# An attention and feed-forward block on one core: all eight PSUM banks in one pool, value products in two halves of the queries, and the normalisation moved from TensorE transposes to transfers and GpSimd

## The chip, the cores and the metric

The kernel runs on one core of a Trainium2 chip. The metric is the device time of one execution in microseconds (us), lower is better. The core has TensorE (PE in the profile, PEld its weight loads), VectorE (DVE), ScalarE (ACT), GpSimd (POOL) and SyncE (SP), which here only issues transfers (DMA). Each engine works through its own list of instructions in order and waits on semaphores for the others. TensorE writes its results into PSUM, which has eight banks of 512 f32 numbers in each of 128 partitions; the other tiles lie in SBUF.

## The reference

For x of 16 batches x 1024 positions x 256 features, with six modulation rows for each batch out of a small product (silu(c) @ w_mod):

```python
h = layernorm(x) * (1 + ca) + sa
Q, K, V = (h @ w.T + b, split into 16 heads of 16)
scores = Q @ K.T / 4 + slope[head] * (k_pos - q_pos), causal
out = softmax(scores) @ V
x = x + ga * (out @ o_w.T + o_b)
h = layernorm(x) * (1 + cb) + sb
gate, y = fp4(h) @ fp4(w_gate).T, fp4(h) @ fp4(w_up).T
x = x + gb * (fp4(silu(gate) * y) @ fp4(w_down).T)
```

fp4 rounds blocks of 16 numbers to a grid of eight magnitudes times the scale of the block. ga and gb are kept at least 0.25 in magnitude.

## The kernel before

The 16 heads are worked on in four groups (g) of four heads (G = 4). For each batch b there are five strands of work, which overlap across batches:

- projections, one batch ahead: N1, N2, N3 (VectorE) normalise x; TR transposes it (TensorE) and ScalarE copies it into featT; U are the query and key projections and V the values. SPL (GpSimd) splits queries and keys into three bf16 parts, and MOVE (SP, six transfers for each unit and group) brings the parts under each other into qa and ka.
- maxima, up to a group ahead: S (TensorE, L655) computes scores with the queries on the partitions, VectorE takes the maximum of each row (L1018, L1020), SM and MT turn the maxima round and TOP (SP) writes them into qa.
- attention: T (L619 to L622) computes the scores again, transposed, ScalarE takes the exponential (L815) into `probs` (three slots in `arena`), and PV (L635) multiplies by the values. The values have a 17th column of ones, so a 17th row of each head's output is the sum of its exponentials. A group has 12 steps (kt, c): kt is one of 8 tiles of keys, c the half of the queries (512 columns); kt of 4 and more meet only c = 1, by causality. Each step issues four products, one for each head, at partitions 0, 32, 64 and 96 of the accumulator `o_acc`, which has two PSUM banks of its own, one for each half.
- after each group: CO (ScalarE, L802) copies o_acc into oT, ON (TensorE, L671) transposes it in eight tiles into two banks, and VectorE takes the reciprocal of the sums (L1044) and multiplies into otok (L1046), which has positions on the partitions. After the fourth group OT (TensorE, L701) transposes otok back in 16 tiles, ScalarE copies it into featT (L834), and O (L711) is the output projection.
- feed forward: LR, LN normalise; XR, XQ, HR, HQ are the fp4 rounding on VectorE and GpSimd (L937, L940), XT and HT transposes, GA (L730), UP (L737) and DN (L753) the three products, RES adds the residual on GpSimd and OUT stores. The residual of the next batch (XIN, FOLD) is loaded into xr behind it.

The order on each engine is written out before the kernel is built: `plan()` adds every job with a cost, a due time and the jobs that it comes after, and `Plan.settle()` puts them one by one, always the one that can start earliest, and among those the one due first. The other six PSUM banks are given out there too: `banks` is how many neighbouring banks a job of TensorE takes, and the job on the other engine that empties them gives them back. Three rings bound how many jobs an engine may have waiting: A (TensorE to ScalarE, four), D (TensorE to VectorE, two) and Q (VectorE to GpSimd, two). A batch is planned at L = 240 us. On the chip `open_banks(e)` waits until the last owners of the banks have emptied them; no job is reordered.

Of the kernel before, what the change touches and what calls it, by code (L numbers as in the profile page):

```python
# [7 lines left out]
ALU = mybir.AluOpType  # L8
# [7 lines left out]
P = 128  # L16
BANK = 512
# [27 lines left out]
STEPS = [(kt, c) for kt in range(T) for c in range(2) if c == 1 or kt < T // 2]  # L45
# [3 lines left out]
NT = len(TILES)  # L49
DIAGONAL = [s for s, (kt, c) in enumerate(STEPS) if c == kt // (T // 2)]  # L50
# [28 lines left out]
class Plan:  # L79
# [5 lines left out]
    BANKS, AHEAD = 6, {"A": 4, "D": 2, "Q": 2}  # L85

    def __init__(self):
        self.jobs, self.order = {}, {e: [] for e in ("PE", "ACT", "DVE", "POOL", "SP")}
        self.bank, self.before = {}, {}

    def add(self, engine, event, cost, due, *after, lag=0.06, ring=None, takes=None, lock=None, banks=0):


        self.jobs[engine, event] = (cost, due, [a for a in after if a], lag, ring, takes, lock, banks)

    def settle(self):
# [29 lines left out]
        while ready:  # L126
# [36 lines left out]
            if banks:  # L163
# [3 lines left out]
                owner[first:first + banks] = [(self.RINGS[ring][1], event)] * banks  # L167
# [15 lines left out]
def plan():  # L183
# [9 lines left out]
    def projections(b, at):  # L193
# [51 lines left out]
    def attention(b, at):  # L245
        n, last = 0, ("PE", ("T", b - 1, NG - 1, NS - 1, jobs_of(NS - 1) - 1))
        for g in range(NG):
            for s in range(NS):
                w = span(s)[1]
                heads = together(s)  # L250
                for i in range(jobs_of(s)):
# [7 lines left out]
                    n += heads  # L259
                p.add("PE", ("PV", b, g, s), 1.9e-3 * w + 0.03, due + 3, ("ACT", ("T", b, g, s, jobs_of(s) - 1)),  # L260
                      ("PE", ("PV", b, g, s - 1)) if s else None, ("ACT", ("CO", b, g - 1) if g else ("CO", b - 1, NG - 1)) if s == 0 else None,
                      ("DVE", ("V", b, 1)) if (g, s) == (0, 0) else None,
                      ("PE", ("ON", b, g - 1) if g else ("ON", b - 1, NG - 1)) if s == NS - 1 else None, lag=0.22)
# [15 lines left out]
    def feed_forward(b, at):  # L279

        for c in range(C):
            for hf in range(2):
                pe(("OT", b, c, hf), 0.55, at + 1.0, ("DVE", ("ON", b, NG - 1)), ("PE", ("V", b + 1, 1)), ring="A", on="ACT",
                   takes_cost=0.59)
        for r in range(NPAIR):
            pe(("O", b, r), 1.75, at + 2.0 + r, ("ACT", ("OT", b, 0, r // 2)), ("ACT", ("OT", b, 1, r // 2)), ("POOL", ("WG", b)),
# [53 lines left out]
def adaln_block(nc, x, wq, bq, wk, bk, wv, bv, wo, bo, w_gu, w_down, cond, w_mod, out):  # L340
    start_slope = 2.0 ** (-8.0 / H)
    slopes = [start_slope * start_slope ** i for i in range(H)]
    rows_dram = nc.dram_tensor("rows_dram", (B, 4 * D), F32).ap()

    with ExitStack() as ctx:
# [7 lines left out]
        o_acc = ctx.enter_context(nc.psum_tensor("o_acc", [P, 2 * BANK], F32))  # L353
# [14 lines left out]
        otok = sb("otok", [P, T, D])  # L368
# [28 lines left out]
        rden = [sb(f"rden{n}", [P, T, G]) for n in range(2)]  # L397
# [7 lines left out]
        wraw2 = otok[:, :, :].rearrange("p t f -> p (t f)")  # L405
# [4 lines left out]
        slope_row = sb("slope_row", [1, 8, H])  # L410
        slope_col = sb("slope_col", [P, H])
        is_a, is_b = sb("is_a", [P, 1]), sb("is_b", [P, 1])
# [7 lines left out]
        o_free = sem("o_free")  # L420
# [36 lines left out]
        def _(sp):  # L457
# [75 lines left out]
            for r in range(NPAIR):  # L533
                sp.wait_ge(stored[r], 16 * B)
# [699 lines left out]
```

## Time and profile before

| | |
|---|---|
| median of 3 runs | 4182.7 us (4179.85 to 4183.4) |
| the profiled execution | 4182.51 us |
| its span, first to last instruction | 4180.7 us |
| mean granted clock of TensorE | 0.967 |
| TensorE busy | 3731.8 us (89%), 22068 matmuls |
| VectorE busy | 3130.8 us (75%) |
| ScalarE busy | 1946.8 us (47%) |
| GpSimd busy | 1196.2 us (29%) |
| bytes moved by transfers | 169.89 MB |

The chain of work that ended last lies for 73% of the span on TensorE, 13% on VectorE and 9% on ScalarE. Busy times of an engine leave out its waits; the busy time of a group of instructions counts overlapping instructions once.

### The profile page before, as it was taken

Reading aid. Unit: us, or ns where it says so; the run is one execution under the profiler, and the core shown is the slowest. Engines: PE = TensorE matmul, PEld = TensorE weight load, DVE = VectorE, ACT = ScalarE, POOL = GpSimd, SP = SyncE. Lnnn points to the kernel's source line nnn. Section 1 sums busy time; section 2 is a strip of 40 time slices with the busy share of each in tenths; the row PEclk is TensorE's granted clock in tenths of the full one; section 3 lists DMA queues with packets and bytes.
Section 4 is the critical chain, followed back from the end, with each engine's and each line's share of the span. In section 5 each row is a group of like instructions: output and inputs, shape, how many; then the busy total and the mean of one; then the engine's idle time right before and its main releaser. Section 6 shows DMA issues by size and latency. Waiting matters only on the chain.

```text
span 4180.7 us, 58634 instructions
## 1 busy us (share of the span) xinstructions
PE 3731.8 (89%) x22068; PEld 1974.5 (47%) x22068; DVE 3130.8 (75%) x6125; ACT 1946.8 (47%) x3535; POOL 1196.2 (29%) x886
## 2 busy tenths in 40 slices
PE   1799999999989989999999999999999998999886
PEld 0334454454545445454544545445454544544445
DVE  7477768778786787877777786777877688776855
ACT  2255444544444554444444454454544455445441
POOL 2222314132231323223132331423224132321223
PEclk6799999999999999999999999999999999999997
DMA  2532122213122122212213122222212212212000
GB/s 76 71 57 33 39 43 45 40 34 51 30 48 45 28 46 41 49 34 46 43 29 52 34 44 46 37 41 37 51 31 52 46 25 49 41 27 45 11 15 10
DMA packets 127981, 169.89 MB, mean 41 GB/s; under 512 B 22020, under 2 KB 75988, under 8 KB 127700
## 3 DMA queue, kind: packets, MB, share of 16 engines
q1 hardware_dynamic: 127700, 166.15, 22.8%
q8 instruction: 176, 2.88, 0.3%
q14 instruction: 105, 0.86, 0.1%
HBM read 47.01 MB, written 16.84 MB: 15 GB/s over the span
## 4 chain that ended last, share of the span: by engine, by line
PE 73%; DVE 13%; ACT 9%; issue 2%; SPq 1%; DMA 1%; POOL 1%; DVEq 0%; ACTq 0%; POOLq 0%
PE o_acc L635 13%; PE banks L655 10%; PE banks L619 9%; PE banks L753 8%; PE banks L730 7%; PE banks L737 7%; ACT arena L815 7%; PE banks L686 4%; PE banks L711 3%; PE banks L694 3%; PE banks L746 2%; DVE banks L1020 2%; DVE tm L993 2%; PE banks L622 1%; PE banks L671 1%
## 5 line engine op out<-in xcount | busy, mean ns | idle before, releaser
L815 ACT ACTIVATE arena<-banks 128x512 f32<-128x512 f32 (+1 forms) x2432 | 1289.4, 576 | 1239.7 <-PE banks L622 702.9
L1020 DVE CUSTOM_DVE_ANT_0 banks<-banks,mask 128x640 f32<-128x640 f32 (+3 forms) x1024 | 1038.0, 1040 | 228.1 <-PE banks L655 218.3
L619 PE MATMUL banks<-qa,ka 105*128 105x512 bf16 (+3 forms) x3072 | 852.3, 332 | 154.3 <-ACT arena L815 125.4
L655 PE MATMUL banks<-ka,qa 102*128 102x512 bf16 (+3 forms) x3072 | 761.6, 334 | 104.7 <-DVE top L1020 80.1
L635 PE MATMUL o_acc<-arena,va 128*17 128x512 f32 (+3 forms) x6144 | 642.4, 500 | 13.1 <-ACT arena L815 12.5
L619 PEld LDWEIGHTS banks<-qa,ka 105*128 105x128 bf16 x3072 | 280.2, 98 | 674.1 <-ACT arena L815 471.2
L655 PEld LDWEIGHTS banks<-ka,qa 102*128 102x128 bf16 x3072 | 267.1, 99 | 484.8 <-DVE top L1020 150.9
L1018 DVE TENSOR_REDUCE top<-banks 128x2 f32<-128x768 f32 (+3 forms) x384 | 391.6, 1043 | 138.5 <-PE banks L660 107.8
L937 POOL TENSOR_TENSOR hid<-hid,tm 128x704 f32<-128x704 f32 x128 | 214.7, 1678 | 900.1 <-DVE hid L994 900.1
L753 PE MATMUL banks<-wdT,hqT 128*128 128x256 f32 x1536 | 371.2, 393 | 3.6 <-ACT hqT L846 3.2
L730 PE MATMUL banks<-wguT,xqT 128*128 128x352 f32 x1024 | 337.0, 463 | 2.8 <-ACT hqT L846 2.0
L737 PE MATMUL banks<-wguT,xqT 128*128 128x352 f32 x1024 | 328.4, 464 | 1.6 <-DVE top L1020 1.2
L753 PEld LDWEIGHTS banks<-wdT,hqT 128*128 128x128 f32 x1536 | 293.4, 195 | 73.6 <-ACT hqT L846 15.1
L622 PE MATMUL banks<-maskT,identb 128*128 128x128 bf16 x1536 | 323.4, 222 | 0.0
L945 POOL TENSOR_TENSOR xr<-xr,delta 128x256 f32<-128x256 f32 x128 | 93.0, 727 | 615.7 <-DVE delta L1123 615.7
L841 ACT ACTIVATE hid<-banks 128x352 f32<-128x352 f32 x256 | 118.5, 463 | 305.7 <-PE banks L730 305.3
L1117 DVE TENSOR_TENSOR hid<-hid,banks 128x704 f32<-128x704 f32 x128 | 113.5, 887 | 191.6 <-PE banks L737 181.9
L737 PEld LDWEIGHTS banks<-wguT,xqT 128*128 128x128 f32 x1024 | 189.3, 190 | 106.6 <-DVE top L1020 4.2
L730 PEld LDWEIGHTS banks<-wguT,xqT 128*128 128x128 f32 x1024 | 183.0, 191 | 100.7 <-ACT hqT L846 6.5
L635 PEld LDWEIGHTS o_acc<-arena,va 128*17 128x17 f32 x6144 | 108.2, 96 | 251.7 <-issue 147.9
L937 POOL TENSOR_TENSOR xb<-xb,tm 128x512 f32<-128x512 f32 x64 | 81.3, 1270 | 457.8 <-DVE xb L994 457.8
L1123 DVE TENSOR_TENSOR delta<-banks,ffn_rows 128x256 f32<-128x256 f32 x128 | 54.2, 423 | 199.9 <-PE banks L753 137.0
(148 smaller groups left out, 4929.5 us busy)
## 6 DMA issues: line engine op xcount, KB each, us to landing
qa<-parts SPq DMA_DIRECT2D x384, 128.0 KB, 4.6
ka<-parts SPq DMA_DIRECT2D x384, 128.0 KB, 6.2
xa<-in_x SPq DMA_DIRECT2D x16, 1024.0 KB, 5.2
xr<-in_x SPq DMA_DIRECT2D x64, 256.0 KB, 2.8
out_x<-xr SPq DMA_DIRECT2D x64, 256.0 KB, 2.1
ffn_rows<-rows_dram SPq DMA_DIRECT2D x16, 384.0 KB, 4.2
ga_row<-rows_dram SPq DMA_DIRECT2D x16, 128.0 KB, 2.9
qa<-in_w_mod SPq DMA_DIRECT2D x2, 768.0 KB, 5.6
```

Source lines behind the costliest of these rows:

```text
L619: mm = pe.matmul(ps[:, m * w:(m + 1) * w], ka[g][0:KT, h, kt * P:(kt + 1) * P], qa[g][0:KT, h, q0:q0 + w], start=heads < G, stop=heads == ...
L622: mm = pe.matmul(ps[:, m * w:m * w + P], identb[:, :], maskT[:, :], start=False, stop=True, skip_group_check=True)
L635: mm = pe.matmul(o_acc[32 * h:32 * h + VW, q0:q0 + w], va[:, kt, g * G + h, :], probs[:, s % P_SLOTS, h, 0:w], start=(kt == 0), stop=(kt = ...
L655: mm = pe.matmul(ps[:, at:at + z - a], qa[g][0:KS, h0 + m, qt * P:(qt + 1) * P], ka[g][0:KS, h0 + m, a:z], start=qt > 0, stop=qt == 0 or h ...
L686: mm = pe.matmul(ps[:, :], w[:, c, m * P:(m + 1) * P], featT[:, c, hf * BANK:(hf + 1) * BANK], start=(c == 0), stop=(c == C - 1))
L730: mm = pe.matmul(ps[:, 0:FH], src[:, c, :], wguT[:, c, e[3] * FH:(e[3] + 1) * FH], start=(c == 0), stop=(c == C - 1))
L737: mm = pe.matmul(ps[:, k * BANK:k * BANK + FH], src[:, c, :], wguT[:, c, FF + k * FH:FF + (k + 1) * FH], start=(c == 0), stop=(c == C - 1))
L753: mm = pe.matmul(ps[:, 0:D], hqT[t % 2][:, c, :], wdT[:, c, :], start=(c == 0), stop=(c == FC - 1))
L815: nc.scalar.activation(probs[:, s % P_SLOTS, j * heads:(j + 1) * heads, 0:w], ps[:, 0:heads * w].rearrange("p (h q) -> p h q", h=heads), A ...
L937: nc.gpsimd.tensor_tensor(u, u, m, ALU.subtract).then_inc(gridded, 1)
L1018: nc.vector.tensor_reduce(tops, ps, AX.X, ALU.max).then_inc(d_free, 1)
L1020: nc.vector.tensor_tensor_reduce(out=ps, in0=ps, in1=mask[:, S - w:S], scale=1.0, scalar=MASKED, op0=ALU.add, op1=ALU.max, accum_out=tops) ...
```

## The change

PSUM: `o_acc` is gone, `banks` has all eight. A half of the queries takes one bank with its first PV (`FIRST`) and holds it until its own copy CO (`holder`) has been made after its last PV (`LAST`). The steps run first over the four tiles of keys of half 0, then over the eight of half 1. Ring D may have three jobs waiting, and the maxima are due 30 us ahead instead of 20.

Normalisation: ON and OT go, and with them otok and its reciprocals. oT keeps the features on the partitions, as O needs them. For each group SP issues DEN (the four rows of sums out of oT into 128 partitions x 32), VectorE takes the reciprocal (RD), SP writes them to DRAM (RDW) and reads them back spread over 64 partitions (RBC, into rsumT); NUM, four transfers, brings the 4 x 16 rows of outputs together in onT. For each two groups GpSimd multiplies onT by rsumT (MUL, 128 x 1024). O reads onT and waits for both MULs of the batch. CO waits until DEN and NUM of the group before have landed. O no longer reads featT, and TR no longer waits for an earlier O.

At the start VectorE clears all eight banks first, where it cleared o_acc, and the first transposes wait for it; some small tiles of the start share space.

```diff
-STEPS = [(kt, c) for kt in range(T) for c in range(2) if c == 1 or kt < T // 2]
+STEPS = [(kt, c) for c in range(2) for kt in range((c + 1) * T // 2)]
+FIRST, LAST = (0, T // 2), (T // 2 - 1, NS - 1)
...
-    BANKS, AHEAD = 6, {"A": 4, "D": 2, "Q": 2}
+    BANKS, AHEAD = 8, {"A": 4, "D": 3, "Q": 2}
...
-                owner[first:first + banks] = [(self.RINGS[ring][1], event)] * banks
+                owner[first:first + banks] = [self.holder[event]] * banks
...
-                pe(("TR", b, c, hf), 0.5, at + 0.08 * L + c, ("DVE", ("N3", b, 1)), ("PE", ("O", b - 2, NPAIR - 1)),
-                   ("PE", ("V", b - 1, 1)), ring="A", on="ACT", takes_cost=0.8)
+                pe(("TR", b, c, hf), 0.5, at + 0.08 * L + c, ("DVE", ("N3", b, 1)), ("PE", ("V", b - 1, 1)), ring="A", on="ACT", takes_cost=0.8)
...
-                due = at + L * n / (NG * sum(h * (q + 1) * P for q, _, h in TILES)) - 20.0
+                due = at + L * n / (NG * sum(h * (q + 1) * P for q, _, h in TILES)) - 30.0
...
-            p.add("ACT", ("CO", b, g), 1.2, due, ("PE", ("PV", b, g, NS - 1)))
-            pe(("ON", b, g), 1.2, due + 6, ("ACT", ("CO", b, g)), ("PE", ("OT", b - 1, C - 1, 1)), ring="D", on="DVE",
-               takes_cost=1.15, banks=2, then=(("DVE", ("ON", b, g - 1)),) if g else ())
+                      banks=1 if s in FIRST else 0, holder=("ACT", ("CO", b, g, c)) if s in FIRST else None)
+                if s in LAST:
+                    past = (b, g - 1) if g else (b - 1, NG - 1)
+                    p.add("ACT", ("CO", b, g, c), 0.6, due, ("PE", ("PV", b, g, s)), ("SP", ("NUM", *past)), ("SP", ("DEN", *past)))
+            normalise(b, g, due)
+
+    def normalise(b, g, due):
+
+        old = (b, g - 1) if g else (b - 1, NG - 1)
+        done = [("ACT", ("CO", b, g, c)) for c in range(2)]
+        p.add("SP", ("DEN", b, g), 0.7, due, *done, ("DVE", ("RD", *old)), lag=2.5)
+        p.add("SP", ("NUM", b, g), 2.6, due + 1, *done, ("PE", ("O", b - 1, NPAIR - 1)), lag=3.0)
+        p.add("DVE", ("RD", b, g), 0.4, due, ("SP", ("DEN", b, g)), ("SP", ("RDW", *old)))
+        p.add("SP", ("RDW", b, g), 0.7, due, ("DVE", ("RD", b, g)), ("SP", ("RBC", *old)), lag=2.5)
+        p.add("SP", ("RBC", b, g), 0.7, due, ("SP", ("RDW", b, g)), ("POOL", ("MUL", b, g // 2 - 1) if g >= 2 else ("MUL", b - 1, C - 1)), lag=3.0)
+        if g % 2:
+            p.add("POOL", ("MUL", b, g // 2), 2.2, due + 10.0, *((("SP", (k, b, n)) for n in (g - 1, g) for k in ("NUM", "RBC"))))
...
+                        sp.dma_start(sums[:, :], oT[HD:P:P // G, :]).then_inc(sums_in, 16)
...
+                        for h in range(G):
+                            sp.dma_start(onT[half + HD * h:half + HD * (h + 1), g // 2, :],
+                                         oT[P // G * h:P // G * h + HD, :]).then_inc(outputs_in, 16)
...
+                    sp.dma_start(rsum_dram[g].rearrange("h (p q) -> (h p) q", q=G * S // P), rsums[:, :]).then_inc(rsums_out, 16)
...
+                    sp.dma_start(rsumT[half:half + 64, :], rsum_dram[g].unsqueeze(1).broadcast_to((G, HD, S))).then_inc(rsumT_in, 16)
...
-                            mm = pe.matmul(o_acc[32 * h:32 * h + VW, q0:q0 + w], va[:, kt, g * G + h, :],
-                                           probs[:, s % P_SLOTS, h, 0:w], start=(kt == 0),
-                                           stop=(kt == (c + 1) * (T // 2) - 1), skip_group_check=True)
+                            mm = pe.matmul(out[32 * h:32 * h + VW, :], va[:, kt, g * G + h, :],
+                                           probs[:, s % P_SLOTS, h, 0:w], start=s in FIRST,
+                                           stop=s in LAST, skip_group_check=True)
...
                         if r == 0:
+                            pe.wait_ge(normal, b * C + C)
                             pe.wait_ge(wog_ready, b + 1)
...
-                                mm = pe.matmul(ps[:, j * D:(j + 1) * D], featT[:, c, t * P:(t + 1) * P], wog[:, c, :],
+                                mm = pe.matmul(ps[:, j * D:(j + 1) * D], onT[:, c, t * P:(t + 1) * P], wog[:, c, :],
...
-                        act.wait_ge(pv_done, (b * NG + e[2] + 1) * NS)
-                        for c in range(2):
-                            nc.scalar.copy(oT[:, c * BANK:(c + 1) * BANK], o_acc[:, c * BANK:(c + 1) * BANK]).then_inc(o_free, 1)
+                        _, _, g, c = e
+                        n = b * NG + g
+                        act.wait_ge(pv_done, n * NS + LAST[c] + 1)
+                        if n:
+                            act.wait_ge(outputs_in, 64 * n)
+                            act.wait_ge(sums_in, 16 * n)
+                        nc.scalar.copy(oT[:, c * BANK:(c + 1) * BANK], bank(("PV", b, g, FIRST[c]))).then_inc(o_free, 1)
...
+                        nc.gpsimd.tensor_tensor(onT[:, c, :], onT[:, c, :], rsumT[:, :], ALU.mult).then_inc(normal, 1)
...
+            nc.vector.memset(banks[:, :], 0.0).then_inc(banks_clear, 1)
...
-            step(nc.vector.memset(o_acc[:, :], 0.0))
```

## Rows read from the trace of the kernel before

**Rows 1.** The page, part 1: busy us of each engine.

```profile
PE 3731.8 (89%) x22068; PEld 1974.5 (47%) x22068; DVE 3130.8 (75%) x6125; ACT 1946.8 (47%) x3535; POOL 1196.2 (29%) x886
```

**Rows 2.** Two stretches: length, busy PE, PEld, DVE, ACT, POOL, clock, DMA, GB/s.

```profile
184.20:4037.30 3853.10, 3561.79 (x21475) 1869.44 (x21475) 2935.10 (x5666) 1892.14 (x3454) 1100.53 (x807) 0.99 0.23 40
...
4037.30:4180.70 143.40, 96.56 (x356) 70.70 (x355) 84.57 (x150) 20.62 (x43) 42.15 (x34) 0.81 0.05 14
```

**Rows 3.** TensorE's waits: us in total, times, longest.

```profile
PE banks L619 <- ACT arena L815: 125.4, 300, 1.0
PE banks L655 <- DVE top L1020: 80.1, 48, 4.5
```

**Rows 4.** Groups by line and form: count, busy us, mean ns, idle before.

```profile
L671 PE MATMUL banks<-ident,oT 128*128 128x128 f32 x512 | 75.5, 295 | 1.9 <-DVE va L1065 0.9 <-ACT arena L815 0.8 <-DVE top L1020 0.2
...
L701 PE MATMUL banks<-ident,otok 128*128 128x128 f32 x256 | 31.4, 276 | 1.3 <-DVE otok L1046 1.3
...
L1046 DVE TENSOR_TENSOR otok<-banks,rden 128x512 f32<-128x512 f32 x64 | 44.2, 691 | 2.2
...
L1044 DVE RECIPROCAL rden<-banks 128x32 f32<-128x32 f32 x64 | 22.9, 357 | 14.5 <-PE banks L671 13.3
```

**Rows 5.** The timeline of TensorE, batch border near 2090: start, length, instruction.

```profile
2092.16 1.04 PE L671 MATMUL banks<-ident,oT 128*128 128x128 f32 x8
2093.13 0.45 PE L655 MATMUL banks<-ka,qa 102*128 102x512 bf16 x2
...
2095.35 1.97 PE L701 MATMUL banks<-ident,otok 128*128 128x128 f32 x16
2097.15 0.49 PE L655 MATMUL banks<-ka,qa 102*128 102x512 bf16 x2
...
2097.70 2.60 PE L711 MATMUL banks<-wog,featT 128*128 128x256 f32 x11
```

**Rows 6.** Groups by line and form, GpSimd.

```profile
L903 POOL TENSOR_TENSOR xa<-xa,parts 128x1024 f32<-128x1024 f32 x64 | 139.3, 2176 | 5.3
```

**Rows 7.** The instructions of L1095: shortest, median, longest ns.

```profile
L1095 DVE SCALAR_TENSOR_TENSOR xb<-xb,rs,ffn_rows x128: 471/483/2232, 361.2 to 4117.0; 128x256 f32<-128x256 f32 x128
```

**Rows 8.** Groups by line and form, ScalarE's exponentials.

```profile
L815 ACT ACTIVATE arena<-banks 128x512 f32<-128x512 f32 x1920 | 1059.9, 599 | 863.4 <-PE banks L619 467.4 <-PE banks L622 334.6 <-PE o_acc L635 51.5
...
L815 ACT ACTIVATE arena<-banks 128x384 f32<-128x384 f32 x512 | 235.2, 490 | 376.3 <-PE banks L622 368.4
```

**Rows 9.** The copies out of o_acc: all of them, and one pair in ScalarE's timeline.

```profile
L802 ACT COPY oT<-o_acc x128: 574/592/618, 226.2 to 4037.3; 128x512 f32<-128x512 f32 x128
...
2074.84 1.07 ACT L802 COPY oT<-o_acc 128x512 f32<-128x512 f32 x2 [1.25 <-PE o_acc L635]
```

**Rows 10.** SP's timeline around the same border: start and length of the issues.

```profile
2072.99 5.05 SPq L527 DMA_DIRECT2D qa<-parts  x6
2078.13 3.77 SPq L527 DMA_DIRECT2D ka<-parts  x6
```

**Rows 11.** The transfers out of parts (MOVE): issue ns and landing us, shortest, median, longest.

```profile
L527 SPq DMA_DIRECT2D qa<-parts x384: 559/597/1982, 118.1 to 3816.8; - x192
...
DMA to landing us min/median/max: 3.2/5.0/21.5
```

**Rows 12.** DMA issues: count, KB each, median us from issue to landing.

```profile
ga_row<-rows_dram SPq DMA_DIRECT2D x16, 128.0 KB, 2.9
...
rows_dram<-arena SPq DMA_DIRECT2D x4, 16.0 KB, 1.5
```

**Rows 13.** TensorE's timeline at the end: the first output projection.

```profile
4044.31 2.00 PE L711 MATMUL banks<-wog,featT 128*128 128x256 f32 x8 [0.34 <-ACT featT L834]
```

**Rows 14.** The start: the memset of o_acc, SP's issue of slopes, TensorE's first wait.

```profile
L1140 DVE MEMSET o_acc<- 128x1024 f32 x1 | 0.9, 912 | 0.2 <-issue 0.2
...
14.05 0.92 SPq L474 DMA_DIRECT2D slope_col<-slope_row  x1
...
PE banks L565 <- DMA bo_row<-in_bo: 19.2, 1, 19.2
```

More of the change, by code:

```diff
@@ L84, with add @@
     RINGS = {"A": ("PE", "ACT"), "D": ("PE", "DVE"), "Q": ("DVE", "POOL")}
-    BANKS, AHEAD = 6, {"A": 4, "D": 2, "Q": 2}
+    BANKS, AHEAD = 8, {"A": 4, "D": 3, "Q": 2}
     def __init__(self):
         self.jobs, self.order = {}, {e: [] for e in ("PE", "ACT", "DVE", "POOL", "SP")}
-        self.bank, self.before = {}, {}
-    def add(self, engine, event, cost, due, *after, lag=0.06, ring=None, takes=None, lock=None, banks=0):
+        self.bank, self.before, self.holder = {}, {}, {}
+    def add(self, engine, event, cost, due, *after, lag=0.06, ring=None, takes=None, lock=None, banks=0, holder=None):
         self.jobs[engine, event] = (cost, due, [a for a in after if a], lag, ring, takes, lock, banks)
+        if banks:
+            self.holder[event] = holder or (self.RINGS[ring][1], event)
     def settle(self):
@@ L279, in feed_forward @@
     def feed_forward(b, at):
[L281 to L284, printed above, removed]
         for r in range(NPAIR):
-            pe(("O", b, r), 1.75, at + 2.0 + r, ("ACT", ("OT", b, 0, r // 2)), ("ACT", ("OT", b, 1, r // 2)), ("POOL", ("WG", b)),
+            pe(("O", b, r), 1.75, at + 2.0 + r, ("POOL", ("MUL", b, 0)), ("POOL", ("MUL", b, 1)), ("POOL", ("WG", b)),
                ring="D", on="DVE", takes_cost=2.0, then=(("POOL", ("FOLD", b, r)), ("DVE", ("LN", b - 1, NPAIR - 1))))
@@ L531, in _ @@
                     sp.dma_start(qa[g][KS:KT, :, :], topT[g % 2][:, :]).then_inc(top_in[g], 16)
+                elif kind in ("DEN", "NUM"):
+                    g = e[2]
+                    n = b * NG + g
+                    sp.wait_ge(o_free, 2 * n + 2)
+                    if kind == "DEN":
+                        if n:
+                            sp.wait_ge(rsums_ready, n)
+                        sp.dma_start(sums[:, :], oT[HD:P:P // G, :]).then_inc(sums_in, 16)
+                    else:
+                        if b:
+                            sp.wait_ge(d_full, in_d["O", b - 1, NPAIR - 1])
+                        half = 64 * (g % 2)
+                        for h in range(G):
+                            sp.dma_start(onT[half + HD * h:half + HD * (h + 1), g // 2, :],
+                                         oT[P // G * h:P // G * h + HD, :]).then_inc(outputs_in, 16)
+                elif kind == "RDW":
+                    g = e[2]
+                    n = b * NG + g
+                    sp.wait_ge(rsums_ready, n + 1)
+                    if n:
+                        sp.wait_ge(rsumT_in, 16 * n)
+                    sp.dma_start(rsum_dram[g].rearrange("h (p q) -> (h p) q", q=G * S // P), rsums[:, :]).then_inc(rsums_out, 16)
+                elif kind == "RBC":
+                    g = e[2]
+                    half = 64 * (g % 2)
+                    sp.wait_ge(rsums_out, 16 * (b * NG + g + 1))
+                    if g >= 2:
+                        sp.wait_ge(normal, b * C + g // 2)
+                    elif b:
+                        sp.wait_ge(normal, b * C)
+                    sp.dma_start(rsumT[half:half + 64, :], rsum_dram[g].unsqueeze(1).broadcast_to((G, HD, S))).then_inc(rsumT_in, 16)
             for r in range(NPAIR):
@@ L554, in open_banks @@
                         pe.wait_ge(sem, done)
+                copied = [(o[1] * NG + o[2]) * 2 + o[3] + 1 for o in PLAN.before[e] if o and o[0] == "CO"]
+                if copied:
+                    pe.wait_ge(o_free, max(copied))
                 return bank(e)
@@ L561, in setup @@
                         ps = open_setup(e)
+                        pe.wait_ge(banks_clear, 1)
                         pe.wait_ge(ident_set, 4)
@@ L941, in run @@
                                                 ALU.mult).then_inc(quant_done, 1)
+                    elif kind == "MUL":
+                        c = e[2]
+                        n = b * NG + 2 * c + 2
+                        pool.wait_ge(outputs_in, 64 * n)
+                        pool.wait_ge(rsumT_in, 16 * n)
+                        nc.gpsimd.tensor_tensor(onT[:, c, :], onT[:, c, :], rsumT[:, :], ALU.mult).then_inc(normal, 1)
                     elif kind == "RES":
```

71 lines of the change are left out of this document (27 added, 44 removed).

## The prediction

> **What bounds the kernel now.** I read the shares of the engines first [rows 1]: TensorE is busy for 89% of the span, VectorE 75%, ScalarE 47%, GpSimd 29%. A share over the whole span mixes stages, so the stretches come next [rows 2]. From the first value product at 184.2 us to the last copy of an output at 4037.3 us TensorE works 3561.8 of 3853.1 us (92%) and stands still for 291 us. The closing stretch of 143 us is another regime: TensorE is busy for 97 us there, and a chain through all engines sets the end. So in the long middle a microsecond of TensorE work is worth almost a microsecond, and at the end only the length of the chain counts.
>
> Third, the waits of TensorE [rows 3]. Two large ones are waits for a PSUM bank: 125.4 us for ScalarE's exponentials before the scores of L619, in 300 small pieces, and 80.1 us for VectorE's maxima before those of L655, in 48 pieces of 1.7 us. The rest are setup or a few us each. These 205 us are all that more banks could give back.
>
> **The transposes that go.** "ON" (8 transposes for each of 64 groups, L671) and "OT" (16 for each batch, L701) leave TensorE. Their groups are busy for 75.5 and 31.4 us [rows 4]. In the timeline a block of 8 spans 1.04 us, but the next matmul starts 0.97 us after it (2092.16 to 2093.13); 16 span 1.97 and free the engine after 1.80 [rows 5]. So I take off 64 x 0.07 = 4.5 and 16 x 0.17 = 2.7 us: 71.0 + 28.7 = 99.7 us of real occupation. The busy sum holds the dearer blocks at a lower clock too. The last ON and OT (2.8 us) stand in the closing chain and are counted there, so 97 us come out of the middle. Bounds: 0 if idle time takes their place, 107 if the overlap at the end were all cost. I take 97, since TensorE is busy for 92% there.
>
> VectorE loses the reciprocal (22.9 us) and the multiplication out of PSUM (44.2 us) and gets 64 reciprocals of 128x32, the same size as L1044, 0.36 us each: 23 us [rows 4]. ScalarE, busy for 47%, loses the 64 copies of OT. Neither is the bound, so I book nothing; the cover is TensorE's own queue, and without it at most 44 us of VectorE would count. TR, the transposes of a batch's normalised input, no longer waits for an O two batches back, since O leaves featT; among TensorE's large waits [rows 3] there is none for featT: nothing. The value products keep their 12 steps and their widths in another order, and the exponentials stay as many: nothing.
>
> **The multiplications on GpSimd.** 32 tensor products of 128x1024 f32 are added. The nearest row is L903, 2.18 us each: 70 us on an engine busy for 29% [rows 1, 6]. Hidden, as long as nobody stands behind them. They have a side effect that rows show: VectorE's L1095 takes 483 ns in the median and up to 2232 ns [rows 7], which is as long as one GpSimd product more. If each of the 32 held VectorE for its whole length it would cost VectorE 32 x 2.18 = 70 us, and the 40 us of recovered maxima waits (below) would be gone: 4110 instead of 4070. By the typical duration of L1095 it is nearly nothing, and I keep 4070. The Trainium skill (SBUF — State Buffer, "SBUF: two separate sides") says that VectorE, with two SBUF inputs or in a two-port mode, and GpSimd take a shared pair of ports as an exclusive lock for a whole instruction; the maximum of the row agrees with it, its median says that it seldom strikes.
>
> **The banks.** The pool of 6 banks and the fixed 2 of o_acc become one pool of 8; the half with queries 0 to 511 is done first, so a value accumulator is held for 4 steps, then another for 8: mostly one bank, sometimes two, which leaves nearly seven for scores, and ON no longer takes two. The score ring of VectorE may be three deep instead of two, that of ScalarE stays four. Gain between 0 and 205 us [rows 3]. I take half of the 80 us of VectorE's waits, 40 us, and none of the 125: those small pieces are TensorE catching up with exponentials of 0.6 us each [rows 8], which a bank more doesn't make faster.
>
> **The new waits.** SP gets, for each group, DEN (1 transfer), NUM (4), RDW (1), RBC (1): 7 more beside some 15, 28 more in a batch. They stand in SP's single queue with MOVE, TOP, XIN and OUT.
>
> First place: the copy of the first half (CO, c = 0) of a group waits until the last group's DEN and NUM have landed; behind it on ScalarE stand the exponentials, and TensorE waits for those. Groups end every (4037.3 - 226.2)/63 = 60.5 us [rows 9]. The first half holds 7 exponentials of 512 and 4 of 384, 7 x 0.60 + 4 x 0.49 = 6.2 us of the group's (1059.9 + 235.2)/64 = 20.2 us [rows 8], 30%, so its copy is due about 18.4 us after the group's start. Before that SP issues one or two MOVEs (3.8 to 5.1 us each, and at 2072.99 to 2081.90 both in a row [rows 10]), DEN at 0.8, NUM at 4 x 0.6 = 2.4 (a transfer of MOVE takes 0.60 of issue), and a landing of 5.0 us, the median of parts [rows 11]: 12 to 17 us. It fits, by 1.4 to 6 us. Bounds: 0, and with the longest landing of 21.5 us some 15 us once. I take 5 us in all.
>
> Second place: O of a batch waits for the last MUL, and behind O stands everything on TensorE. The chain from the copy is DEN 3.2 (the shortest landing of parts), reciprocal 0.36, RDW 1.5, RBC about 3.6 (256 KB; between ga_row's 2.9 at 128 KB and the 5.0 of parts in a queue), MUL 2.2, and 0.4 for hand-overs: 11.2 us [rows 4, 6, 11, 12], plus 4 to 9 for MOVEs on SP and up to 6.5 for a split on GpSimd. Today the group of 2074.84 has its O only at 2097.70, 22 us after the copy ended at 2075.91 [rows 5, 9], since V and others go first. 15 to 26 us against 22: covered or slightly late. Bounds 0 and 4 us in each of 15 batches; I take 1, so 15 us. The wait of VectorE for DEN stands before its maxima; an engine with a quarter of its time free carries it, 0.
>
> **The ends.** In the closing stretch the copies end at 4037.9 and O starts at 4044.31 [rows 9, 13]: 6.4 us. The new chain takes 11.2, and one copy instead of two follows the last product (-0.5): +4 us. At the start the memset covers 4096 columns instead of 1024, some 3.65 us instead of 0.91, ahead of the slopes; but SP is busy with weights until 14.05 us and TensorE waits for the biases until 19.2 us [rows 14]: nothing.
>
> **The sum.** The profiled execution took 4182.5 us (span 4180.7, 1.8 around it), the median of the runs is 4182.7. 4182.5 - 97 - 40 + 5 + 15 + 4 = 4069.5, say 4070 us.
>
> **Rivals.**
> 1. The banks give much more. For it: TensorE stands still for 291 us in the middle, 205 of them for banks. Against: only one ring gets deeper. With 130 us instead of 40: 3980 us.
> 2. O comes late. For it: three transfers in series, and on GpSimd's queue a split may stand ahead. Against: the 22 us of cover. At 6 us instead of 1 for each of 15 batches: 4145 us.
> 3. The change doesn't do what it says: idle time takes the place of the transposes, because exponentials and maxima pace the middle. For it: the 300 waits for ScalarE. Against: 92% busy. 97 and 40 fall away: 4180 to 4200 us, no change.
> 4. The other side: the copy of the first half holds ScalarE in every group, since NUM lands behind two MOVEs. For it: the margin of 1.4 us in the worse order, and landings up to 21.5 us. Against: copies that are due later when the first half is stretched. At 3.5 us in each of 63 groups, 220 us, less the 5 booked: 4285 us. It decides from 118/63 = 1.9 us a group.
>
> **How the numbers follow.** Chances: the forecast 0.52 (its own range 4030 to 4115), rival 1 0.13, rival 2 0.11, rival 3 0.10, rival 4 0.14. The range reaches from 4000, between rival 1 and the forecast, to 4180, which takes in rival 2 and the edge of rival 3; rival 4 and the lowest part of rival 1 are left out, about 0.2. 0.2% (8 us) is about what a measurement of this kernel can tell from no change. Faster: forecast, rivals 1 and 2, 0.76. Same: most of rival 3, 0.08. Slower: rival 4 and the rest, 0.16.
>
> **What would show it.** In the profile after: TensorE's busy time near 3630 us; its waits for L1020 near 40 and for L815 near 125 us; hardly a wait of L711 (O) for GpSimd and of ScalarE's copy for a DMA; groups every 59 us; O about 11 us after the last copy at the end. A long idle of ScalarE before the copy of the first half, released by a transfer out of oT, means rival 4; TensorE idle before O released by GpSimd, rival 2; unchanged spacing of groups with more idle everywhere, rival 3. The weakest step is the 40 us: nothing in the trace shows what one bank more is worth, or what another written order of the queues does.

## The result and the profile after

The changed kernel takes 4133.4 us in the median (4130.7 to 4138.7), the kernel before 4181.3 in the same runs: ratio 0.9888, interval 0.9871 to 0.9905. It is 48 us faster, where 111 were forecast. That 4133 lies in the forecast's range is luck: the two halves of the change, measured apart below, missed what was booked for them by 155 and by 220 us, in opposite directions. Nor does one written order settle the sign: planned at L = 242, the changed kernel took 30 us more than the kernel before at its 240 (last runs below).

Part 1 of the page of the changed kernel, and TensorE's two stretches (columns as in [rows 2]):

```profile
PE 3628.4 (88%) x21300; PEld 1919.7 (46%) x21300; DVE 3058.5 (74%) x6061; ACT 1912.8 (46%) x3471; POOL 1279.1 (31%) x918
```

```profile
182.00:3974.90 3792.90, 3456.99 (x20715) 1815.74 (x20715) 2858.48 (x5600) 1859.90 (x3393) 1181.33 (x839) 0.97 0.30 49
3974.90:4129.80 154.90, 92.91 (x320) 67.34 (x320) 83.48 (x148) 18.01 (x38) 44.16 (x35) 0.76 0.07 17
```

TensorE is busy for 103 us less than in [rows 1]: the 107 us of ON and OT [rows 4] went, O's matmuls rose by 30 and the others fell by 26. But it stands still for 3792.9 - 3457.0 = 336 us in the middle, where it was 291 [rows 2], and the granted clock of the middle fell from 0.99 to 0.97. The work went, and idle time and a slower clock came.

TensorE's largest waits after (beside [rows 3]):

```profile
PE banks L753 <- issue: 143.5, 16, 17.3
PE banks L671 <- ACT arena L861: 50.9, 139, 0.9
PE banks L708 <- DVE top L1066: 38.1, 19, 3.5
```

The waits for banks fell from 125 to 51 and from 80 to 38 us. In their place stands one in front of O (now L753), once in each batch: 8.4 us in the mean of the 15 in the middle, and 17.3 us in the closing stretch. "issue" means only that the profile has no instruction that released it just then; the code has one wait in that place, for `normal`, which MUL raises. The timeline of TensorE at one border:

```profile
2051.13 0.54 PE L708 MATMUL banks<-ka,qa 102*128 102x512 bf16 x2
2060.39 8.66 PE L753 MATMUL banks<-wog,onT 128*128 128x256 f32 x32 [8.71 <-issue]
```

and its windows (length, busy PE, granted clock, DMA share, GB/s):

```profile
2040.00:2051.70 11.70, 11.67 (x64) 1.00 0.91 106
2051.70:2060.40 8.70, 0.01 (x1) 0.78 0.11 30
2060.40:2069.00 8.60, 8.60 (x33) 0.82 0.37 109
```

The stall is followed by a stretch at 0.82 of the full clock: part of it at the lower of the two levels, 1.2 GHz. (Before the stall, from 2040.00 to 2051.70, TensorE worked without a break at 1.00.) The same matmuls of O were busy for 118.5 us before and are for 148.3 us now.

SP at the same border (start, length of the issue):

```profile
2034.60 3.79 SPq L543 DMA_DIRECT2D qa<-parts  x6
2038.48 0.63 SPq L556 DMA_DIRECT2D sums<-oT  x1
2039.21 2.45 SPq L562 DMA_DIRECT2D onT<-oT  x4
2041.78 4.06 SPq L543 DMA_DIRECT2D ka<-parts  x6
2045.94 0.53 SPq L570 DMA_DIRECT2D rsum_dram<-rsums  x1
2051.53 0.60 SPq L579 DMA_DIRECT2D rsumT<-rsum_dram  x1
```

GpSimd and VectorE there:

```profile
2057.95 2.34 POOL L987 TENSOR_TENSOR onT<-onT,rsumT 128x1024 f32<-128x1024 f32 x1 [18.94 <-DMA rsumT<-rsum_dram]
```

```profile
2043.68 0.35 DVE L1090 RECIPROCAL rsums<-sums 128x32 f32<-128x32 f32 x1 [3.70 <-DMA sums<-oT]
```

Read together: the copy ended at 2036.34. DEN waited for a MOVE and was issued at 2038.48; its sums were there at 2043.68, 5.2 us after the issue. RDW waited behind the next MOVE until 2045.94, RBC until RDW had landed, 5.6 us, MUL until RBC had, 6.4 us. O starts 24 us after the copy, and so it does at all 15 borders of the middle (23.2 to 24.4 us). TensorE had come to O 15.3 us after the copy. The plan gives these landings 2.5, 2.5 and 3.0 us. And as `settle()` lets a job of the same engine start at the end of the other's issue, it gives RBC no landing of RDW at all. The landings, taken from the semaphore events of the trace, differ by the group's place in its batch: DEN 2.1 to 3.0 us in the first group, mostly 7.0 to 7.7 in the second, 3.7 to 5.5 at the border; RDW 1.4 to 3.4 in the first two groups and mostly 4.1 to 6.0 in the last two; RBC mostly 9.7 to 11.0 in the first and 5.7 to 6.8 in the last two. Around this border the DMA engines were busy for 91% (first window above).

The chain doesn't hold TensorE alone. VectorE stands before RD for 144 us, GpSimd before MUL for 448 us (64 of them in one piece) with RES, FOLD and WG behind it in its list. VectorE's and GpSimd's waits after:

```profile
DVE rsums L1090 <- DMA sums<-oT: 115.6, 33, 7.4
...
DVE rsums L1090 <- issue: 28.6, 14, 4.1
```

```profile
POOL onT L987 <- DMA rsumT<-rsum_dram: 447.7, 32, 64.1
```

ScalarE's copies, which the prediction feared for (rival 4), hardly wait for a transfer: 3.7 us, once. At the end the last copy ends at 3974.98 and O starts at 3991.59, 16.6 us later where it was 6.4.

### The profile page after: what moved, and what is told of

Same layout as the page of the kernel before. It is cut to its first block, busy times and chain, and to the rows that moved or that the text cites. A ratio compares the mean times of both kernels' runs of the same rounds, so it can differ in the third digit from the quotient of the medians.

```text
span 4129.8 us, 57832 instructions
## 1 busy us (share of the span) xinstructions
PE 3628.4 (88%) x21300; PEld 1919.7 (46%) x21300; DVE 3058.5 (74%) x6061; ACT 1912.8 (46%) x3471; POOL 1279.1 (31%) x918
## 4 chain that ended last, share of the span: by engine, by line
PE 67%; ACT 7%; issue 6%; DVE 6%; DMA 5%; SPq 5%; POOL 4%; POOLq 0%; ACTq 0%; DVEq 0%
PE banks L688 11%; PE banks L708 9%; PE banks L671 8%; PE banks L795 8%; PE banks L772 7%; PE banks L779 7%; ACT arena L861 4%; SPq L543 4%; PE banks L733 4%; DMA sums<-oT 4%; PE banks L753 3%; PE banks L741 3%; PE banks L788 2%; DVE banks L1066 2%; PE banks L674 1%
## 5 line engine op out<-in xcount | busy, mean ns | idle before, releaser
L671 PE MATMUL banks<-qa,ka 105*128 105x512 bf16 (+3 forms) x3072 | 833.4, 331 | 92.3 <-ACT arena L861 50.9
L688 PE MATMUL banks<-arena,va 128*17 128x512 f32 (+3 forms) x6144 | 648.1, 497 | 20.7 <-ACT arena L861 16.4
L779 PE MATMUL banks<-wguT,xqT 128*128 128x352 f32 x1024 | 328.7, 464 | 0.0
L772 PE MATMUL banks<-wguT,xqT 128*128 128x352 f32 x1024 | 327.2, 465 | 1.3 <-ACT xqT L879 0.7
L753 PE MATMUL banks<-wog,onT 128*128 128x256 f32 x512 | 148.3, 460 | 143.5 <-issue 143.5
L688 PEld LDWEIGHTS banks<-arena,va 128*17 128x17 f32 x6144 | 105.5, 95 | 258.4 <-ACT arena L861 126.7
L987 POOL TENSOR_TENSOR onT<-onT,rsumT 128x1024 f32<-128x1024 f32 x32 | 76.8, 2401 | 447.7 <-DMA rsumT<-rsum_dram 447.7
L888 ACT COPY hqT<-banks 128x512 f32<-128x512 f32 (+1 forms) x256 | 110.9, 482 | 214.0 <-PE banks L788 213.8
```

What stands on the lines that cost most here:

```text
L671: mm = pe.matmul(ps[:, m * w:(m + 1) * w], ka[g][0:KT, h, kt * P:(kt + 1) * P], qa[g][0:KT, h, q0:q0 + w], start=heads < G, stop=heads == ...
L688: mm = pe.matmul(out[32 * h:32 * h + VW, :], va[:, kt, g * G + h, :], probs[:, s % P_SLOTS, h, 0:w], start=s in FIRST, stop=s in LAST, ski ...
L753: mm = pe.matmul(ps[:, j * D:(j + 1) * D], onT[:, c, t * P:(t + 1) * P], wog[:, c, :], start=(c == 0), stop=(c == C - 1))
L772: mm = pe.matmul(ps[:, 0:FH], src[:, c, :], wguT[:, c, e[3] * FH:(e[3] + 1) * FH], start=(c == 0), stop=(c == C - 1))
L779: mm = pe.matmul(ps[:, k * BANK:k * BANK + FH], src[:, c, :], wguT[:, c, FF + k * FH:FF + (k + 1) * FH], start=(c == 0), stop=(c == C - 1))
```

## The experiments

All beside the kernel before, at 4181.5 to 4183.1 us in the same runs. Each is the changed kernel ("after"), the kernel before, or banks_only, with the edit shown. Most edits of the plan also write out another order of the engines; the three runs at the end measure what that alone does.

**banks_only**: after, with ON, OT, the reciprocal and multiplication out of PSUM (L1044, L1046) and O's reading of featT put back as before; CO waits for ON of the group before.

> One part of the change alone: eight banks in one pool, halves of the queries, ring D three deep, maxima due 30 us ahead; the transposes ON and OT and their normalisation stay as before. From the waits after (TensorE for exponentials 125 to 51 us, for maxima 80 to 38): if these belong to the banks alone, 4181 - 117 = about 4065 us. By the prediction's own term, 40 us: 4140 us. Rival (the waits fell only because TensorE lost time before O instead, the banks give nothing): 4180 us.

Measured 3986.8 us (3985.2 to 3988.4), ratio 0.9538 (0.9522 to 0.9554): 195 us faster than before and 147 faster than the change. None of the three expected times was met, and the banks gave nearly five times what the prediction booked. TensorE's waits in banks_only (L1031 and L1029 are the L1020 and L1018 of the kernel before):

```profile
PE banks L628 <- ACT arena L828: 64.0, 166, 0.9
...
PE banks L665 <- DVE top L1029: 8.8, 17, 0.7
...
PE banks L665 <- DVE top L1031: 2.0, 6, 0.4
```

In the kernel before, beside the 80.1 us of L1020 in [rows 3], there was also:

```profile
PE banks L655 <- DVE top L1018: 12.9, 9, 9.7
```

In the middle of banks_only TensorE stands still for 3655.6 - 3491.5 = 164 us, at a clock of 0.99:

```profile
187.00:3842.60 3655.60, 3491.54 (x21422) 1862.34 (x21416) 2847.30 (x5654) 1880.59 (x3449) 1097.51 (x807) 0.99 0.24 42
```

The middle is 197 us shorter than in [rows 2]: 127 us of idle and 70 us of busy time of TensorE went, though it still makes all 22068 matmuls. The mean granted clock of the run rose from 0.967 to 0.973, which is worth some 22 us of the 3562 (an estimate); the other 48 us were not traced.

**norm_only**: before, with the new normalisation; o_acc, six banks, step order, rings and due times of before, CO copying both halves together.

> The other part alone: normalisation by transfers and GpSimd, with o_acc, the six banks, the old order of the steps, rings and due times of before. Transposes saved 97 us; O's stall and its clock cost 9 to 12 us a batch, 140 to 190 us: 4181 - 97 + 165 = about 4250 us, slower than before. Rival (with the old banks TensorE has more other waits in which O's wait is hidden): 4130 us.

Measured 4300.8 us (4297.8 to 4307.7), ratio 1.0291 (1.0276 to 1.0307): 119 us slower. The direction was expected, the loss is 51 us larger. Its wait before O is 102 us. So the change is two edits of opposite sign: -195 and +119 alone. Together they would be -76 if they simply added; measured is -48.

**o_free_of_wait**: after, O reading a constant tile.

```diff
-                            pe.wait_ge(normal, b * C + C)
...
-                                mm = pe.matmul(ps[:, j * D:(j + 1) * D], onT[:, c, t * P:(t + 1) * P], wog[:, c, :],
+                                mm = pe.matmul(ps[:, j * D:(j + 1) * D], wqT[:, c, j * P:(j + 1) * P], wog[:, c, :],
```

> The changed kernel with one edit: O multiplies a constant tile (wqT) in place of the normalised outputs onT, and so doesn't wait for the multiplications on GpSimd; every transfer, reciprocal and multiplication is still made, in the same order. Theory (late O): the 16 stalls of TensorE before O (143.5 us in the trace) go, and with them the slower clock after each (O's matmuls mean 460 ns where they took 384, some 40 us): 4133 - 143 - 40 = about 3950 us. Rival (the time is set by transfers or by VectorE anyway, the stall before O only collects what would be lost elsewhere): 4080 us or more.

Measured 4096.9 us (4094.4 to 4102.9). The theory missed by far, and the rival's 4080 us or more came true: the 143 us of stall gave back only 37, the rest is lost elsewhere. VectorE, in turn, now stands 139 us before its part of O, since it needs FOLD, which is in GpSimd's list behind MUL, and TensorE waits 81 us for that:

```profile
PE banks L708 <- DVE xr L1118: 81.3, 13, 7.6
```

```profile
DVE xr L1118 <- issue: 139.1, 15, 10.7
```

That it is FOLD is read from the code: L1118 waits for `folded`, and "issue" names no releaser. The slow clock moved too. O's matmuls are busy for 113 us only, but the mean clock of the run stayed at 0.95, since after the new stall (7.6 us, to 2060.01) other matmuls run at the lower level (TensorE alone: length, busy, clock, DMA share, GB/s):

```profile
2050.00:2060.00 10.00, 2.38 (x31) 0.85 0.31 92
2060.00:2070.00 10.00, 8.93 (x31) 0.50 0.05 14
```

**mul_o_unwaited**: in addition MUL multiplies two weight tiles without a wait, and NUM lands where nobody reads.

```diff
-                        pool.wait_ge(outputs_in, 64 * n)
-                        pool.wait_ge(rsumT_in, 16 * n)
-                        nc.gpsimd.tensor_tensor(onT[:, c, :], onT[:, c, :], rsumT[:, :], ALU.mult)
+                        nc.gpsimd.tensor_tensor(onT[:, 0, :], wguT[:, 0, 0:S], wguT[:, 1, 0:S], ALU.mult)
```

> The changed kernel with O on a constant tile as before and, in addition, MUL on GpSimd multiplying two constant tiles (weights) without waiting for the transfers NUM and RBC; NUM lands in one half of onT that nobody reads. All transfers and instructions are made, in the same written order. Only VectorE's reciprocal still waits for a transfer (144 us of idle before it in the trace after). Revised theory (late transfers hold three queues in turn: SP feeds them late, then VectorE at RD, GpSimd at MUL with RES, FOLD and WG behind it, TensorE at O): GpSimd's share is what kept O's wait from giving back its time, so 3920 to 4010 us. Rival (the added work itself, or the transfers' traffic, costs): 4070 us or more.

Measured 4023.5 us (4019.8 to 4025.7), another 73 us off, a little above the range expected.

**chain_unwaited**: in addition RD reads a constant tile and doesn't wait for DEN.

```diff
-                        dve.wait_ge(sums_in, 16 * n + 16)
-                        nc.vector.reciprocal(rsums[:, :], sums[:, :])
+                        nc.vector.reciprocal(rsums[:, :], tiniest[:, 0:G * S // P])
```

> As mul_o_unwaited, and VectorE's reciprocal RD reads a constant tile without waiting for DEN: no engine but SP waits for the new transfers, except ScalarE's copies (CO), which keep their wait. Same instructions, transfers and written order. Revised theory: nothing of the new normalisation but hidden work is left, so banks alone less the transposes, 3987 - 99 = about 3890 us, up to 3930 us. Rival (the port shared by VectorE and GpSimd, the traffic, or a written order that is worse whatever the waits): 4000 us or more.

Measured 3983.1 us (3975.6 to 3990.2), another 40 us. With the same number of instructions and the same order, three waits are worth 150 us, taken away one after the other: 37 before O, 73 before MUL, 40 before RD. But this is only level with banks_only, not 99 us below, and between the two times expected. The middle, and two of TensorE's waits:

```profile
184.00:3840.30 3656.30, 3431.49 (x20714) 1788.49 (x20713) 2862.95 (x5601) 1859.00 (x3393) 1180.69 (x839) 0.99 0.31 51
```

```profile
PE banks L712 <- DVE top L1069: 41.0, 37, 2.6
...
PE banks L712 <- DVE xr L1121: 27.0, 13, 3.0
```

The middle is as long as that of banks_only. TensorE is busy for 60 us less in it and idle for 61 us more. All its waits for VectorE's maxima make 61 us, where banks_only has 11, and 27 us are for VectorE's part of O. What VectorE and GpSimd wait for:

```profile
POOL xr L971 <- DMA xr<-in_x: 576.0, 62, 15.9
```

```profile
DVE xr L1121 <- issue: 81.7, 15, 10.3
```

FOLD waits 576 us for XIN, where it is 309 in banks_only: SP stands 201 us before RBC for the landing of RDW in this run (175 in the changed kernel), with OUT and XIN behind it. SP's list is the fourth place where the chain holds somebody. That this accounts for the whole rest was not tried.

**true_lags**: after, with other delays in the plan.

```text
lag of DEN 2.5 -> 5.0, NUM 3.0 -> 4.5, RDW 2.5 -> 5.5, RBC 3.0 -> 6.5
```

> The changed kernel, only the planner's delays of the four kinds of transfers raised to what the trace after shows near a batch's border: DEN 2.5 to 5.0 us, NUM 3.0 to 4.5, RDW 2.5 to 5.5, RBC 3.0 to 6.5. No instruction is added or left out; O moves back in TensorE's written order by some 10 us. Theory (late O): other work of TensorE fills the stall, the idle before O falls from 143 to under 30 us and the clock comes back: 3960 to 4010 us. Rival (nothing else is ready at a batch's border, or the feed-forward strand is then the longest): 4100 us or more.

Measured 4176.1 us (4153.0 to 4189.5): 43 us slower than the change, O still waits 111 us; the rival's 4100 us or more was met. The delay given to RDW had no effect at all, as its follower is on the same engine: `plan()` writes the same order for every engine with 2.5 and with 5.5.

**rdw_only_honest** and **honest_sp**: the first mends that one link with the old delays, the second has the delays of true_lags and ("DEN", "RDW", "OUT") in the place of ("RDW",).

```diff
-                earliest[key2] = max(earliest[key2], t + cost if key2[0] == engine else done[key])
+                earliest[key2] = max(earliest[key2], t + cost if key2[0] == engine and event[0] not in ("RDW",) else done[key])
```

> The changed kernel with one link of the plan mended: RBC is planned after RDW's landing (its own 2.5 us), where the planner took the end of RDW's issue. Delays as in the change. If this missing 2.5 us is the main fault of the order: 4030 to 4070 us. If the too short delays of DEN and RBC matter as much (5.2 and 6.4 us measured against 2.5 and 3.0): 4090 to 4130 us.

> The changed kernel with the planner's delays of true_lags, and one more correction: a job that follows DEN, RDW or OUT on the same queue is planned after the landing, where the planner took the end of the issue (RBC after RDW: 3 to 5.5 us in which SP stands still on the chip and the planner didn't know it). Theory (O, MUL and RD are late because the written order rests on a chain that is too short): TensorE's wait before O falls below 40 us and the time to 4000 to 4060 us. Rival (true_lags, which was slower than the changed kernel, shows that the order isn't at fault; each written order has its own few per cent): 4130 us or more.

Measured 4144.3 us (4138.8 to 4145.2) and 4030.6 us (4028.9 to 4034.2). The first lies above both of its ranges, the second in the theory's. Neither mend alone helps (4144 and 4176 against 4133); the two together, with OUT's link, take 103 us off the change. DEN in the list changes nothing in the written order, and OUT only the lists of GpSimd and SP. With both, the wait before O is 31 us in 6 places:

```profile
PE banks L753 <- issue: 30.5, 6, 18.6
```

**honest_l230**: honest_sp with `L = 230.0`.

> honest_sp with the planner's pace L = 230 instead of 240, so another written order of the same jobs with the same delays. Theory (true delays make the order fit the chip): 3960 to 4040 us, near honest_sp's 4031. Rival (honest_sp was one lucky order): 4090 us or more.

Measured 4082.1 us (4080.0 to 4083.0), between the two times expected. It is 51 us below the change at L = 240. The change itself was not run at L = 230, so how much of this, and of honest_sp's 103 us, the delays gave and how much the order is not shown.

**chain_on_act**: DEN, RDW and RBC on ScalarE's queue (`p.add("ACT", ...)`, `act.dma_start`), landings honoured, delays of the change.

> The changed kernel with DEN, RDW and RBC issued from ScalarE's queue instead of SP's, landings honoured in the plan as in honest_sp, delays as in the change (2.5, 2.5, 3.0). NUM, MOVE and the rest stay on SP. Theory (SP's single queue is the place where the chain is held, behind twelve transfers of MOVE at each group's end, and where it holds OUT and XIN in its turn): landings of DEN fall from 5 to about 3 us, VectorE's wait before RD from 144 to under 50 us, 4000 to 4070 us. Rival (ScalarE now stands where SP stood, and the exponentials with it): 4130 us or more.

Measured 4174.7 us (4164.6 to 4184.2). VectorE's wait before RD fell to 87 us, but O still waits 118 us, and the rival's 4130 us or more was met. The theory that SP's queue alone holds the chain falls.

**banks_d2, banks_due20, steps_only, ring3_only**: one number or line each.

```text
 banks_d2:     BANKS, AHEAD = 8, {"A": 4, "D": 3 -> 2, "Q": 2}      (banks_only)
 banks_due20:  due = ... - 30.0 -> 20.0 of S                 (banks_only)
 steps_only:   STEPS in the new order                        (before)
 ring3_only:   BANKS, AHEAD = 6, {"A": 4, "D": 2 -> 3, "Q": 2}      (before)
```

> banks_only with ring D two deep again instead of three; the pool of eight, the halves and the due times stay. If the deeper ring is what gave the 195 us (VectorE's waits fell from 80 to 9 us): 4080 us or more. If it is the pool with a value accumulator that no longer makes the next group wait: below 4020 us.

> banks_only with the maxima due 20 us ahead, as before the change, instead of 30. If the earlier due time is a piece of the 195 us: 4020 us or more. If it is not: 3987 within 15 us.

> The kernel before with one line changed: the order of the twelve steps, all of half 0 first; o_acc, six banks, rings and due times as before. By the prediction's term (nothing): 4181 us, within 15. Rival (the order alone lets scores and exponentials interleave better and is part of the 195 us): 4140 us or less.

> The kernel before with one number changed: ring D three deep instead of two, on the six banks it has. banks_d2 lay 133 us over banks_only, so the ring is the largest single piece. If a deeper ring alone gives it: 4060 to 4100 us. If it needs the banks of the pool (a score tile of VectorE takes up to two banks, and six banks with four jobs of ring A leave one pair): 4150 us or more.

Measured 4120.1, 4111.0, 4236.4 and 4359.7 us (each within 8 us but for ring3_only, 4358.7 to 4371.1). The times expected if the piece matters were met, but for steps_only, which lies 55 us above its 4181. In the pool the third place in the ring is worth 133 us and the earlier due time 124; without the pool the third place costs 177 us and the new order of the steps 54. So most of the 195 us comes only with the pieces together: the pool, its ring and the time to fill it. Each of these was tried in one written order.

**before_l250, banks_l242, after_l242**: the planner's pace alone.

```diff
-    L = 240.0
+    L = 250.0        (242.0 in the other two)
```

> The kernel before with the planner's pace L = 250 instead of 240, nothing else. The distance to 4182 us is what a written order alone moves: within 40 us if the comparisons above can be read as they stand, 100 us or more if they can't.

> banks_only with the planner's pace L = 242 instead of 240: another written order of the same jobs. If the banks and the deeper ring give the time: 3980 to 4050 us. If 3987 was a lucky order: 4100 us or more.

> The changed kernel with the planner's pace L = 242 instead of 240, the second member of the pair with banks_l242 (4066 us). If the new normalisation costs more than its 99 us of saved transposes whatever the order: 4130 to 4230 us. If its loss was an unlucky order: below 4066 us.

Measured 4168.7 us (4166.3 to 4170.7), 4065.8 (4062.8 to 4068.2) and 4211.4 (4195.6 to 4216.4). An order alone moved before by 14 us and the two others by 79 and 78 us. Expectations were met for before_l250 and after_l242 and missed by 16 us for banks_l242. The pairs agree: in both orders the new normalisation costs over the banks alone 147 us (4133 - 3987) and 146 us (4211 - 4066). The banks give 195 us at L = 240, and 117 at L = 242 against the before of 240. The whole change gives 48 us at L = 240 and costs 30 at L = 242 against the same before: its size, and even its sign, lie within what an order moves.

One thing could have been read before anything ran: `settle()` also adds up the length of its plan (`self.length`). Worked out from each run's kernel.py, it is 4158 us for the kernel before, 3994 for banks_only, 4184 for steps_only, 4141 for banks_d2, 4053 for banks_due20, 4256 for ring3_only, 4131 for before_l250 and 4035 for banks_l242: each within 60 us of the chip, ring3_only within 104. (The chip's start, before the first projections, isn't in the plan.) It has 165 of the banks' 195 us. For the kernels with the new normalisation it is 3866 (the change), 4017 (norm_only) and 3869 (after_l242), which is 267, 284 and 342 us too short; for honest_sp, 3934, it is 97 too short. The plan knows the banks and doesn't know the new chain.

## Why the prediction was right or wrong, point by point

- **The transposes, 97 us**: right as occupation (107 us of busy time of ON and OT are gone), and not had in time: even chain_unwaited, without the three waits, is level with banks_only, with 60 us less busy and 61 us more idle time in the middle.
- **The banks, 40 us**: the term that was most mis-sized. It measured 195 us (117 at another pace). The prediction took the waits for banks as the ceiling of the gain and half of VectorE's as the value. From before to banks_only these two waits fell by 61 + 78 = 139 us, that for L1018 by 4, and all idle of the middle by 291 - 164 = 127 us. That alone is three times the 40; the other 70 us are busy time, which the prediction took as fixed. So "all that more banks could give back" was no ceiling. That the eight banks alone don't give it, banks_d2 and banks_due20 show; how much of it is the written order is not shown (79 us between two orders of banks_only).
- **The new waits, 5 + 15 + 0 us**: the step that failed and turned a large gain into a small one. The first place, ScalarE's copy: right, 3.7 us. The second, O behind MUL: 8.4 us a batch measured, 1 booked. The chain's single parts were priced from light or short landings (3.2, 1.5, 3.6) and measured 5.2, 5.6 and 6.4. With the allowance for MOVEs and a split it was still right as a whole: 24 us from the copy to O, in the 15 to 26 foreseen. What failed is the cover set against it. The 22 us were read off the order of before, but the new plan puts O where its own too short delays let it, 15.3 us after the copy. Booking VectorE's wait before RD at 0 because a quarter of its time is free was wrong by 40 us, and GpSimd's at MUL, for which nothing was booked as long as nobody stands behind it, is the dearest (73 us, in the sequence tried): what stands behind the wait in the list counts, not the share of free time.
- **The clock** was not in the sum. After the stall of 8.7 us TensorE's next 8.6 us had a clock of 0.82; O's busy time rose by 30 us. o_free_of_wait shows that this cost follows the stall and not O.
- **The ends**: the start right (first wait of TensorE 18.9 us, before 19.2); the closing chain 16.6 us instead of 11.2, +10 instead of +4. From the end of the last copy to the end of the span it is 155 us, where it was 143.
- **The shared port**: L1138 (before L1095) has a median of 485 ns and a maximum of 2578 ns, where it had 483 and 2232, but no run tells this part apart from the rest.
- **Rivals**: rival 1 (banks give much more) and rival 2 (O late) both happened, one against the other; rival 2's mechanism was too narrow, as it saw one of four lists. Rival 3's outcome, idle in the transposes' place, came too, but not for its reason alone: most of it goes back to the waits before O, MUL and RD, and with these gone it stands before the maxima (61 us) and VectorE's part of O (27 us). By its own sum it would have been 4207 us, not 4180 to 4200. Rival 4 did not happen.
- **The sum**: the banks gave 155 us more than booked; the normalisation, booked at -97 + 5 + 15 + 4 = -73 us, cost 147 on top of the banks, 220 us off the other way. 4070 - 155 + 220 = 4135: the two misses nearly cancel, and that is luck.

What stays open: why the maxima and VectorE's part of O hold TensorE longer in chain_unwaited (SP's hold of XIN was not tried away); what of the banks' gain is their own and what their order's; RD unwaited alone, which was not tried; and whether the chain would be shorter with transfers of another shape. Of the kernels that compute the whole block, banks_only is the fastest at 3987 us: the pool with the old transposes beats both.

## What to carry to other kernels

Where engines follow lists written out beforehand, a wait costs what stands behind it in that list: trace a late transfer through every in-order queue that it enters, SP's too, before calling it hidden. Price a chain of dependent transfers with landings from stretches where the big transfers run, and let the planner honour them also between two jobs of one queue. Compare the plan's own length with the time measured: here it was a fair forecast until a chain came in that it had too short. When a change joins two edits, measure each alone, and measure one neutral change of the order as well: here it is worth up to 79 us, so a gain below that, such as this change's own 48, belongs to no edit until a second order shows it.

## What the runs showed of the hardware that was not expected

At the border near 2040 a transfer of 16 KB between SBUF tiles (DEN) landed 5.2 us after its issue and one of 16 KB to DRAM (RDW) took 5.6 us, with twelve transfers of 128 KB around them; in the closing stretch, with SP's queue nearly empty, the same two took about 2 us:

```profile
3975.00 0.60 SPq L556 DMA_DIRECT2D sums<-oT  x1
...
3978.88 0.43 SPq L570 DMA_DIRECT2D rsum_dram<-rsums  x1
3980.91 0.58 SPq L579 DMA_DIRECT2D rsumT<-rsum_dram  x1
```

```profile
3977.11 0.35 DVE L1090 RECIPROCAL rsums<-sums 128x32 f32<-128x32 f32 x1 [2.60 <-DMA sums<-oT]
```

The spreading read RBC (256 KB into 64 partitions) took 8.2 us there, until MUL at 3989.15, with two loads issued behind it. Over all groups it took 5.7 to 11.0 us, where the loads of 256 KB into xr took 2.7 us in the median. Another shape of it was not tried. The Trainium skill (DMA: Bandwidth & Descriptors, "Anatomy of one DMA — SWDGE (gpsimd) path") puts the fixed cost of a transfer at about 2 us, mostly the confirmation of its last byte; it says so for transfers issued on GpSimd's path, and these were issued by SP. The two small ones of the closing stretch agree with 2 us, those beside the large transfers are far above it.
